# First stage of a two-layer transformer kernel: two batches ahead of the attention, two along with it

## The chip, the cores and the metric

The kernel runs on one core of a Trainium2 chip. The metric is the device time of one execution in microseconds (us). Before the change it is 1527.2 us, the median of three runs (1524.87 to 1527.45). A measurement of this kind tells about 0.2%, some 3 us, from no change.

PE is the matrix engine, DVE the vector engine, ACT the activation engine, POOL the general engine; SP only issues DMAs here. Each runs its own instructions strictly in order, and they wait for each other by semaphores. PSUM holds eight banks of 512 fp32 per partition, and PE writes there; DVE and ACT read from there.

## The reference

Input x is 4 batches x 1024 tokens x 128. Two transformer layers follow; layer 0 is the one that the change touches:

```python
xn = _ln(x, g_attn, b_attn)
qkv = (xn @ qkv_w + qkv_b)          # 16 heads of 8
scores = einsum('bhqd,bhkd->bhqk', q, k) / sqrt(8)
scores = where(causal, -inf, scores)
attn = einsum('bhqk,bhkd->bhqd', softmax(scores), v)
attn = attn @ out_w + out_b
x = x + attn
# 8 steps of a recurrence with tanh, a second norm, a gelu feed-forward, a linear part,
# then layer 1: attention without a mask, and a relu feed-forward; a norm after each part
```

All of it is computed in fp32 accuracy. For the score products q and k are therefore split in three bf16 parts each.

## The kernel before, in words

**Stages.** The first stage makes q, k and v of layer 0. For each batch it has six steps, in `FIRST_STEPS`: *norm* (DVE takes the statistics of 8 tiles of 128 tokens, `L495`, `L499`), *scale* (POOL takes the root of the variance, `L508` to `L519`; ACT then scales half of the tiles, `L526`, and DVE the other half, `L533`), *turn* (PE transposes, `L545`; ACT copies with gain and bias, `L617`), *q* and *k* (PE multiplies, `L552`; ACT writes the first bf16 part, `L620`, `L625`; DVE the remainder in fp32, `L633`; ACT the second part, `L623`, `L628`; DVE the third, `L638`) and *v* (PE, `L560`, and DVE adds the bias, `L657`). The k product waits for the remainder of q, the v product for that of k, since both use the same bank. SP writes the parts to HBM (`scr_q`, `scr_k`, `L604`), and later loads them in another layout, four heads at a time (`load_group`, `L113`, 14 DMAs: a *load*). There are 16 loads a layer: a batch has four groups of four heads. A load waits until its batch is written.

**Attention.** A group of layer 0 has 20 units. A *max* unit is a score product on PE (`L383`, with the mask's product `L389`) and its row maximum on DVE (`L324`). They run 24 units ahead. When the maxima of half a group's queries are complete, POOL splits them (`L265` to `L271`), PE transposes (`L436`), ACT copies (`L309`), and SP stores them to HBM and loads them as further rows of Q (`L230`, `L235`): that is *turn_max*. A *key* unit is the score product again, keys by queries with the maxima subtracted within the product (`L404`), and the exponential on ACT (`L296`). POOL cuts the diagonal blocks (`L280`). *weigh* multiplies with v (`L426`), *turn_out* transposes back and divides (`L443`, `L342`, `L345`).

**PSUM.** Two of the eight banks collect the weighed values. The other six are a ring of three slots of two banks (`RING`). Each max, key, turn_max and turn_out takes the next slot, and its PE instruction waits in `slot_free` until the entry that had the slot has been read out. The first stage does not use the ring: batch b has slot b (`bank[b]`), the fourth being the two banks of the weighed values.

**Order.** `Program` gives each entry a tick; all engines walk through the same sorted list and take out what is theirs. Before: batch b's step i has tick b + i, then come load 0, 1 and 2, then the attention of layer 0, one key unit a tick. The last ticks of layer 0 have the first steps of the middle stage among them. Batches 1 and 2 of the first stage work in the buffer `shared`, 0 and 3 in `own`. The attention needs `shared` for its exponentials.

## Time and profile before

| | |
|---|---|
| median of the runs | 1527.2 us |
| profiled execution | 1526.45 us |
| its span, first to last instruction | 1524.7 us |
| busy PE / DVE / ACT / POOL | 90% / 82% / 71% / 18% |
| mean granted PE clock | 0.966 |

The times of the rows below count from the start of the span. A row of the order in time is one instruction or several alike in a row; idle time stands in brackets with what ended it. PE's busy time is modelled, since its products overlap. The granted clock is a share of 2.4 GHz; 0.50 is 1.2 GHz. An fp32 product is counted as two instructions (two products of 512 columns are x4).

### The profile page before, as it was taken

The page shows a single profiled execution, that of the slowest core. Times are in us where ns is not written, and L with a number is a line of the kernel's source. Part 1 is how long each engine was busy: PE and PEld are TensorE (multiplying, and loading weights), DVE is VectorE, ACT ScalarE, POOL GpSimd, SP SyncE. Part 2 cuts the span into 40 slices and gives each one's busy share as a digit, 9 for nine tenths or more (in the row PEclk, how much of TensorE's full clock was granted, in tenths as well). Part 3 has the DMA queues.
Part 4 walks back from the last instruction along what each step waited for, and adds up shares of the span by engine and source line. Part 5 has one row for each costly group of instructions (what it writes and reads, how often), then busy time and mean ns, then how long its engine had stood idle before and what let it go on. Part 6 is the DMA issues. An engine that isn't in the chain of part 4 may idle for free.

```text
span 1524.7 us, 31977 instructions
## 1 busy us (share of the span) xinstructions
PE 1369.9 (90%) x13016; PEld 565.3 (37%) x13016; DVE 1249.3 (82%) x1715; ACT 1081.6 (71%) x1239; POOL 278.1 (18%) x624
## 2 busy tenths in 40 slices
PE   6699999999998768888679999999999999999886
PEld 3333434343343334446423333233333333233355
DVE  7978888888885387885989999999999999997143
ACT  6167777777777657764358888888888888887642
POOL 4021322223133132332200000000000000001252
PEclk9689999999999899999889999999999999999998
DMA  5610110101100000012120000000000000000001
GB/s 177 168 45 24 31 38 25 45 24 42 27 4 3 1 1 0 1 65 82 42 64 23 23 24 23 14 17 18 23 23 23 23 23 23 3 3 3 1 15 42
DMA packets 38995, 47.90 MB, mean 31 GB/s; under 512 B 11072, under 2 KB 20160, under 8 KB 38720
## 3 DMA queue, kind: packets, MB, share of 16 engines
q1 hardware_dynamic: 38416, 45.31, 10.1%
q8 instruction: 103, 1.69, 0.4%
q10 hardware_dynamic: 432, 0.53, 0.1%
q14 instruction: 44, 0.36, 0.1%
HBM read 30.22 MB, written 15.47 MB: 30 GB/s over the span
## 4 chain that ended last, share of the span: by engine, by line
PE 62%; DVE 23%; ACT 6%; issue 4%; POOL 3%; SPq 1%; DMA 1%; POOLq 0%; ACTq 0%; DVEq 0%
PE ps L426 22%; DVE l_negp L324 14%; PE ps L404 12%; PE ps L383 12%; PE ps L552 7%; ACT shared L296 3%; PE ps L443 2%; PE ps L389 2%; POOL n_rs L514 2%; DVE n_bst L495 2%; PE ps L545 1%; PE ps L1040 1%; SPq L113 1%; PE ps L908 1%; PE ps L560 1%
## 5 line engine op out<-in xcount | busy, mean ns | idle before, releaser
L324 DVE TENSOR_REDUCE l_negp<-ps 128x2 f32<-128x1024 f32 (+2 forms) x832 | 953.3, 1181 | 75.5 <-PE ps L389 36.4
L296 ACT ACTIVATE shared<-ps 128x1024 f32<-128x1024 f32 (+1 forms) x832 | 820.4, 991 | 196.8 <-PE ps L404 168.1
L426 PE MATMUL ps<-shared,l_vs 128*32 128x256 f32 (+3 forms) x6648 | 515.3, 386 | 4.1 <-POOL shared L280 3.3
L383 PE MATMUL ps<-Ks,Qs 48*128 48x512 bf16 (+3 forms) x1792 | 329.9, 369 | 40.6 <-DVE l_negp L324 27.2
L404 PE MATMUL ps<-Qs,Ks 51*128 51x512 bf16 (+3 forms) x1792 | 320.8, 366 | 25.5 <-ACT shared L296 10.7
L404 PEld LDWEIGHTS ps<-Qs,Ks 51*128 51x128 bf16 x1792 | 81.3, 93 | 330.6 <-issue 159.3
L426 PEld LDWEIGHTS ps<-shared,l_vs 128*32 128x32 f32 x6648 | 134.8, 108 | 172.3 <-issue 141.7
L383 PEld LDWEIGHTS ps<-Ks,Qs 48*128 48x128 bf16 x1792 | 87.6, 94 | 194.3 <-ACT shared L296 91.0
L280 POOL TENSOR_SCALAR_AFFINE_SELECT shared<-shared 128x512 f32<-128x512 f32 x128 | 81.7, 639 | 321.0 <-ACT shared L296 320.9
L265 POOL CAST l_parts<-l_negm 128x16 bf16<-128x16 f32 x64 | 12.6, 197 | 441.8 <-DVE l_negm L329 438.6
L389 PE MATMUL ps<-mask,id 64*128 64x128 bf16 x1024 | 69.2, 223 | 0.0
L552 PE MATMUL ps<-shared,w_sb 128*128 128x512 f32 x120 | 60.8, 639 | 7.6 <-ACT shared L998 5.7
L514 POOL TENSOR_TENSOR n_rs<-n_ve,neg_half 128x4 f32<-128x4 f32 x56 | 62.7, 1120 | 4.4
L552 PE MATMUL ps<-own,w_sb 128*128 128x512 f32 x120 | 61.1, 635 | 2.2 <-DVE attn_tm L849 1.8
L389 PEld LDWEIGHTS ps<-mask,id 64*128 64x128 bf16 x1024 | 50.2, 99 | 21.0 <-issue 2.1
L251 POOL COPY l_vs<-v_tm 128x256 f32<-128x256 f32 x32 | 12.7, 397 | 232.7 <-PE ps L426 199.8
L508 POOL TENSOR_TENSOR n_ve<-n_mv,eps 128x4 f32<-128x4 f32 x56 | 12.2, 218 | 215.4 <-DVE n_mv L499 215.4
L342 DVE RECIPROCAL l_rc<-ps 128x16 f32<-128x16 f32 x64 | 16.5, 257 | 39.7 <-PE ps L443 39.1
L309 ACT ACTIVATE l_msp<-ps 48x128 bf16<-48x128 bf16 x64 | 17.3, 270 | 39.6 <-PE ps L436 39.5
L824 DVE SCALAR_TENSOR_TENSOR own<-own 128x1024 f32<-128x1024 f32 x16 | 19.5, 1219 | 31.1 <-ACT own L767 31.1
L443 PE MATMUL ps<-ident,l_outT 128*128 128x128 f32 x256 | 41.8, 286 | 2.5 <-ACT l_outT L302 2.5
L552 PE MATMUL ps<-own,wx 128*128 128x512 f32 x56 | 31.9, 699 | 12.0 <-DVE own L824 11.8
(160 smaller groups left out, 1090.4 us busy)
## 6 DMA issues: line engine op xcount, KB each, us to landing
Qs<-scr_q SPq DMA_DIRECT2D x128, 64.0 KB
Ks<-scr_k SPq DMA_DIRECT2D x64, 96.0 KB
Qs<-scr_q SPq DMA_DIRECT2D x128, 32.0 KB
Ks<-scr_k SPq DMA_DIRECT2D x64, 64.0 KB
scr_q<-own SPq DMA_DIRECT2D x4, 768.0 KB, 3.6
scr_q<-shared SPq DMA_DIRECT2D x4, 768.0 KB, 3.5
scr_k<-own SPq DMA_DIRECT2D x4, 768.0 KB, 5.0
scr_k<-shared SPq DMA_DIRECT2D x4, 768.0 KB, 4.8
```

What stands on the lines that cost most here:

```text
L280: pool.affine_select(out=blk, in_=blk, compare_op=ALU.is_ge, fill=0.0, base=0, pattern=[[0, GH], [1, P]], channel_multiplier=-1).then_inc( ...
L296: act.activation(dst, src, ACT.Exp, scale=SCALE).then_inc(exped, 1)
L324: dve.tensor_reduce(dst, src, AX_X, ALU.max, negate=True).then_inc(reduced, 1)
L383: last = pe.matmul(outs[par], Qs[s][r:r + MROW, h2, qt * P:(qt + 1) * P], Ks[s][r:r + MROW, h2, at:at + w], start=True, stop=True)
L389: last = pe.matmul(outs[par][:, w - P:w], id2[r:r + ROWS, j, :], mask2[r:r + ROWS, j, :], start=False, stop=True, skip_group_check=True)
L404: last = pe.matmul(to[:, par, i * w:(i + 1) * w], Ks[s][r:r + MROW + 3, h2, kt * P:(kt + 1) * P], Qs[s][r:r + MROW + 3, h2, qh * CH + lo:( ...
L426: last = pe.matmul(pv_ps[q % 2][32 * h:32 * h + 32, a:a + wide], vs[g % 2][:, kt, h, :], pT[m % PRING][:, h, a:a + wide], start=m == u.fir ...
L443: last = pe.transpose(to[:, t * P:(t + 1) * P], outT[:, t * P:(t + 1) * P], ident)
L495: last = dve.bn_stats(self.bst[:, b, t, :], src[:, t * P:(t + 1) * P])
L514: pool.tensor_tensor(self.rs[:, b, of], self.ve[:, b, of], self.norms.neg_half[:, of], ALU.pow)\
L552: last = pe.matmul(bank[:, i * CH:(i + 1) * CH], weight, src[:, i * CH:(i + 1) * CH], start=start, stop=True, skip_group_check=not start)
L824: dve.scalar_tensor_tensor(out=then, in0=u[b], scalar=DT * DT / BETA ** (k + 1), in1=then, op0=ALU.mult, op1=ALU.add).then_inc(moved[b % 2 ...
```

## The change

Batches 0 and 1 are made ahead of the attention, batch 1 two ticks behind batch 0. Batches 2 and 3 are made within it: their six steps have the ticks 60, 64, 68, 72, 76, 80 and 120, 124, ... 140 of the attention of layer 0, each ahead of the attention's entries of that tick. Tick 60 is the first key unit of group 3, tick 120 that of group 6; batch 2's first load is asked for at tick 106, batch 3's at 186. The four PSUM results of a batch (turn, q, k, v) take a slot of the ring each, in turn. All batches work in the two halves of `own`: batch 2 waits until batch 0's are written. A group's load of three groups on is issued at its seventh key unit instead of its first.

```diff
-            if entry[1] == u.first_unit[g] and g % NGRP + 3 < NGRP:
+            if entry[1] == u.first_unit[g] + 6 and g % NGRP + 3 < NGRP:
...
+        if place.before[entry][0] == "first":
+            _, name, b = place.before[entry]
+            if name == "turn":
+                pe.wait_ge(handed.x_ready, b + 1)
+            elif name == "v":
+                pe.wait_ge(handed.v_made[0], b + 1)
+            else:
+                pe.wait_ge(handed.rest["qk".index(name)], b + 1)
+            return
...
-    xT = [work[b][:, 3, :] for b in range(B)]
-    parts = [parts_of(work[b]) for b in range(B)]
+    xT = [work[b % 2][:, 3, :] for b in range(B)]
+    parts = [parts_of(work[b % 2]) for b in range(B)]
...
+            if b >= 2:
+                act.wait_ge(v_mm, b - 1)
             act.wait_ge(n_turned, b + 1)
-            act.activation(xT[b], bank[b], ACT.Identity, bias=C("b_attn"), scale=C("g_attn")).then_inc(x_ready, 1)
+            act.activation(xT[b], bank_of("first", name, b), ACT.Identity, bias=C("b_attn"), scale=C("g_attn")).then_inc(x_ready, 1)
         elif name == "q":
+            if b >= 2:
+                act.wait_ge(written[b - 2], 32)
...
     def tensor(pe, name, b):
+        if name in FIRST_BANKS:
+            bank_free(pe, ("first", name, b))
...
+FIRST_AT = {2: 60, 3: 120}
...
-        out = [(b + i, 0, -b, ("first", name, b)) for i, name in enumerate(FIRST_STEPS) for b in range(B)]
-        at = len(FIRST_STEPS) + B
+        out = [(2 * b + i, 0, -b, ("first", name, b)) for i, name in enumerate(FIRST_STEPS) for b in range(2)]
+        at = len(FIRST_STEPS) + 4
...
+        out += [(at + FIRST_AT[b] + 4 * i, 0, 0, ("first", name, b)) for i, name in enumerate(FIRST_STEPS)
+                for b in range(2, B)]
...
-            elif entry[0] in ("key", "max", "turn_max", "turn_out"):
+            elif entry[0] in ("key", "max", "turn_max", "turn_out") or entry[0] == "first" and entry[1] in FIRST_BANKS:
```

On DVE, the last instructions of the first stage and the first reduce, before (`L633` remainder, `L638` third part, `L657` v):

```order
L633 SCALAR_TENSOR_TENSOR attn_tm<-ps,c_sb,own 128x1024
L638 TENSOR_TENSOR shared<-attn_tm,shared 128x1024
L633 SCALAR_TENSOR_TENSOR v_tm<-ps,c_sb,shared 128x1024
L638 TENSOR_TENSOR shared<-v_tm,shared 128x1024
L657 TENSOR_TENSOR v_tm<-ps,r_sb 128x1024
L638 TENSOR_TENSOR own<-attn_tm,own 128x1024
L633 SCALAR_TENSOR_TENSOR v_tm<-ps,c_sb,own 128x1024
L638 TENSOR_TENSOR shared<-v_tm,shared 128x1024
L657 TENSOR_TENSOR v_tm<-ps,r_sb 128x1024
L638 TENSOR_TENSOR own<-v_tm,own 128x1024
L657 TENSOR_TENSOR v_tm<-ps,r_sb 128x1024
L324 TENSOR_REDUCE l_negp<-ps 128x2x2 x2
```

and with the change, where `L643`, `L648` and `L667` are the same three:

```order
L643 SCALAR_TENSOR_TENSOR v_tm<-ps,c_sb,own 128x1024
L643 SCALAR_TENSOR_TENSOR attn_tm<-ps,c_sb,own 128x1024
L648 TENSOR_TENSOR own<-v_tm,own 128x1024
L667 TENSOR_TENSOR v_tm<-ps,r_sb 128x1024
L648 TENSOR_TENSOR own<-attn_tm,own 128x1024
L643 SCALAR_TENSOR_TENSOR v_tm<-ps,c_sb,own 128x1024
L648 TENSOR_TENSOR own<-v_tm,own 128x1024
L667 TENSOR_TENSOR v_tm<-ps,r_sb 128x1024
L324 TENSOR_REDUCE l_negp<-ps 128x2x2 x2
```

Of the work of four batches that of two is left ahead of the first reduce.

On PE, around the seventeenth unit of group 3, before (`L404` key, `L383` max, `L389` mask, `L426` weigh; `l_reduced` counts DVE's maxima, `exped` ACT's exponentials):

```order
L426 MATMUL ps<-shared,l_vs 32x256 [waits exped]
L426 MATMUL ps<-shared,l_vs 32x256 x3
L404 MATMUL ps<-Qs,Ks 128x384 [waits l_reduced]
L404 MATMUL ps<-Qs,Ks 128x384
L383 MATMUL ps<-Ks,Qs 128x128 [waits exped,loaded0_1]
L383 MATMUL ps<-Ks,Qs 128x128
L389 MATMUL ps<-mask,id 128x128 x4
L383 MATMUL ps<-Ks,Qs 128x128 x2
L389 MATMUL ps<-mask,id 128x128 x4
L426 MATMUL ps<-shared,l_vs 32x256 x4
L404 MATMUL ps<-Qs,Ks 128x384 [waits l_reduced]
L404 MATMUL ps<-Qs,Ks 128x384
```

and with the change (`L411`, `L390`, `L396`, `L433` are these, `L555` is the k product of batch 2; `q_rest0` and `k_rest0` count DVE's remainders):

```order
L555 MATMUL ps<-own,w_sb 128x512 [waits q_rest0,l_reduced]
L555 MATMUL ps<-own,w_sb 128x512
L411 MATMUL ps<-Qs,Ks 128x384 [waits exped]
L411 MATMUL ps<-Qs,Ks 128x384
L390 MATMUL ps<-Ks,Qs 128x128 [waits l_reduced,loaded0_1]
L390 MATMUL ps<-Ks,Qs 128x128
L396 MATMUL ps<-mask,id 128x128 x4
L390 MATMUL ps<-Ks,Qs 128x128 x2
L396 MATMUL ps<-mask,id 128x128 x4
L433 MATMUL ps<-shared,l_vs 32x256 x4
L411 MATMUL ps<-Qs,Ks 128x384 [waits k_rest0]
L411 MATMUL ps<-Qs,Ks 128x384
```

The k product stands in one slot of the ring, and the second key product behind it waits for DVE's remainder of k.

On ACT, in the first units of group 3, before (`L296` exponential, `L302` copy of the weighed values, `L309` maxima):

```order
L296 ACTIVATE shared<-ps 128x2x384 [waits weighed,keyed] x2
L302 ACTIVATE l_outT<-ps 128x512 [waits l_out_turned,weighed]
L296 ACTIVATE shared<-ps 128x2x2x256 [waits weighed,keyed]
L296 ACTIVATE shared<-ps 128x2x2x128 [waits weighed,keyed]
L309 ACTIVATE l_msp<-ps 48x128 [waits l_max_stored,l_max_turned]
```

and with the change, where `L529` is the scaling of batch 2 and `n_shifted` counts POOL's results:

```order
L296 ACTIVATE shared<-ps 128x2x384 [waits weighed,keyed] x2
L302 ACTIVATE l_outT<-ps 128x512 [waits l_out_turned,weighed]
L529 ACTIVATE attn_tm<-x_tm,n_shift,n_rs 128x128 [waits n_shifted]
L529 ACTIVATE attn_tm<-x_tm,n_shift,n_rs 128x128 x3
L296 ACTIVATE shared<-ps 128x2x2x256 [waits weighed,keyed]
L296 ACTIVATE shared<-ps 128x2x2x128 [waits weighed,keyed]
L309 ACTIVATE l_msp<-ps 48x128 [waits l_max_stored,l_max_turned]
```

The exponentials of the fifth and sixth unit come behind a wait for POOL.

## Rows read from the trace of the kernel before

**Rows 1.** Page, part 2: PE and its granted clock, tenths, 40 slices.
```profile
PE   6699999999998768888679999999999999999886
...
PEclk9689999999999899999889999999999999999998
```

**Rows 2.** Busy time by stretch: us, us on each engine (instructions), clock, DMA.
```profile
60.00:74.00 14.00, 9.41 (x81) 3.81 (x75) 13.96 (x15) 0.27 (x1) 0.83 (x4) 0.50 0.51 85
100.00:126.77 26.77, 25.31 (x338) 10.66 (x334) 23.02 (x26) 20.10 (x25) 7.06 (x17) 1.00 0.11 33
```

**Rows 3.** PE in order of time: start, us, what, idle time before.
```profile
17.89 3.62 PE L552 MATMUL ps<-own,w_sb 128*128 128x512 f32 x4
...
47.50 0.29 PE L383 MATMUL ps<-Ks,Qs 48*128 48x128 bf16 x2
...
74.05 0.61 PE L404 MATMUL ps<-Qs,Ks 51*128 51x512 bf16 x2 [1.27 <-DMA Qs<-scr_m]
...
103.39 0.39 PE L404 MATMUL ps<-Qs,Ks 51*128 51x512 bf16 x2
...
210.49 0.39 PE L404 MATMUL ps<-Qs,Ks 51*128 51x512 bf16 x2
```

**Rows 4.** SP's queue in order of time, start of the program.
```profile
35.14 0.36 SPq L604 DMA_DIRECT2D scr_k<-own  x1
39.88 3.09 SPq L113 DMA_DIRECT2D Qs<-scr_q  x8
...
66.54 0.32 SPq L230 DMA_DIRECT2D scr_m<-l_msp  x1
```

**Rows 5.** DVE in order of time, the first row maxima.
```profile
49.58 5.81 DVE L324 TENSOR_REDUCE l_negp<-ps 128x4 f32<-128x512 f32 x6
```

**Rows 6.** Groups by line, 0 to 49.5 us: busy, mean ns; idle before.
```profile
L514 POOL TENSOR_TENSOR n_rs<-n_ve,neg_half 128x4 f32<-128x4 f32 x8 | 8.1, 1014 | 0.6
...
L495 DVE BATCH_NORM_STATS2 n_bst<-x_tm 128x6 f32<-128x128 f32 x32 | 6.8, 278 | 1.4 <-DMA x_tm<-in_x 1.4
L526 ACT ACTIVATE attn_tm<-x_tm,n_shift,n_rs 128x128 f32<-128x128 f32 x16 | 6.6, 482 | 7.6 <-POOL n_shift L519 7.6
...
L657 DVE TENSOR_TENSOR v_tm<-ps,r_sb 128x1024 f32<-128x1024 f32 x4 | 4.9, 1225 | 0.4
L533 DVE TENSOR_SCALAR attn_tm<-x_tm,n_mv,n_rs 128x128 f32<-128x128 f32 x16 | 4.8, 364 | 0.0
...
L499 DVE BATCH_NORM_AGGREGATE n_mv<-n_bst 128x2 f32<-128x6 f32 x32 | 3.0, 158 | 0.3
...
L633 DVE SCALAR_TENSOR_TENSOR attn_tm<-ps,c_sb,own 128x1024 f32<-128x1024 f32 x2 | 2.6, 1279 | 3.4 <-ACT own L620 3.4
...
L638 DVE TENSOR_TENSOR own<-attn_tm,own 128x1024 bf16<-128x1024 f32 x2 | 2.4, 1216 | 0.0
...
L620 ACT ACTIVATE own<-ps,c_sb 128x1024 bf16<-128x1024 f32 x2 | 2.2, 1113 | 3.0 <-PE ps L552 3.0
...
L508 POOL TENSOR_TENSOR n_ve<-n_mv,eps 128x4 f32<-128x4 f32 x8 | 1.6, 206 | 4.4 <-DVE n_mv L499 4.4
```

**Rows 7.** ACT in order of time, batch 0's normalized tokens transposed.
```profile
14.84 1.20 ACT L617 ACTIVATE own<-ps,c_sb 128x1024 f32<-128x1024 f32 x1 [0.45 <-PE ps L545]
```

**Rows 8.** PE in order of time, two key products in mid group.
```profile
227.09 0.39 PE L404 MATMUL ps<-Qs,Ks 51*128 51x512 bf16 x2
...
228.32 0.39 PE L404 MATMUL ps<-Qs,Ks 51*128 51x512 bf16 x2
```

**Rows 9.** DVE in order of time, the same place.
```profile
227.86 4.96 DVE L324 TENSOR_REDUCE l_negp<-ps 128x2 f32<-128x1024 f32 x4 [0.27 <-PE ps L383]
```

**Rows 10.** PE in order of time, products of the middle stage within attention.
```profile
473.87 1.09 PE L545 MATMUL ps<-ident,attn_tm 128*128 128x128 f32 x8
...
478.72 1.98 PE L552 MATMUL ps<-own,w_sb 128*128 128x512 f32 x4
```

**Rows 11.** Groups by line of ACT, 0 to 520 us: table loads.
```profile
L526 ACT ACT_TABLE_LOAD x1 | 1.3, 1283 | 2.2 <-issue 2.2
```

More of the change, by code:

```diff
@@ L285, in scalar @@
             g, m, pairs = u.key_unit[entry[1]]
-            lo, layer = u.step[m][3], g // NGRP
-            if entry[1] == u.first_unit[layer * NGRP]:
-                act.wait_ge(handed.written[layer][1], 32)
-                act.wait_ge(handed.written[layer][2], 32)
-                act.wait_ge(handed.v_mm[layer], 3)
+            lo = u.step[m][3]
+            if entry[1] == u.end[0]:
+                act.wait_ge(handed.written[1][1], 32)
+                act.wait_ge(handed.written[1][2], 32)
+                act.wait_ge(handed.v_mm[1], 3)
             act.wait_ge(keyed, entry[1] + 1)
@@ L361, in slot_free @@
             pe.wait_ge(normed, i + 1)
-        elif kind == "first":
-            pe.wait_ge(handed.v_made[0], i + 1)
         elif kind == "mid":
@@ L594, in first_stage @@
     ln = RowNorm(ctx, nc, norms, 0)
-    n_turned, x_ready = sem("n_turned"), sem("x_ready")
-    s_mm, s_first, s_rest, s_second = ([sem(f"{s}_{n}") for s in "qk"] for n in "mm first rest second".split())
+    n_turned, x_ready, s_rest = sem("n_turned"), handed.x_ready, handed.rest
+    s_mm, s_first, s_second = ([sem(f"{s}_{n}") for s in "qk"] for n in "mm first second".split())
     s_parted, v_mm, v_made, written = handed.parted[0], handed.v_mm[0], handed.v_made[0], handed.written[0]
@@ L615, in scalar @@
                 act.wait_ge(small_in, 32)
+            if b >= 2:
+                act.wait_ge(v_mm, b - 1)
             act.wait_ge(n_turned, b + 1)
-            act.activation(xT[b], bank[b], ACT.Identity, bias=C("b_attn"), scale=C("g_attn")).then_inc(x_ready, 1)
+            act.activation(xT[b], bank_of("first", name, b), ACT.Identity, bias=C("b_attn"), scale=C("g_attn")).then_inc(x_ready, 1)
         elif name == "q":
+            if b >= 2:
+                act.wait_ge(written[b - 2], 32)
             act.wait_ge(s_mm[0], b + 1)
-            act.activation(parts[b][:, 0, 0, :], bank[b], ACT.Identity, bias=C("bq0")).then_inc(s_first[0], 1)
+            act.activation(parts[b][:, 0, 0, :], bank_of("first", name, b), ACT.Identity, bias=C("bq0")).then_inc(s_first[0], 1)
         elif name == "k":
@@ L624, in scalar @@
             act.wait_ge(s_mm[1], b + 1)
-            act.activation(parts[b][:, 1, 0, :], bank[b], ACT.Identity, bias=C("bk0")).then_inc(s_first[1], 1)
+            act.activation(parts[b][:, 1, 0, :], bank_of("first", name, b), ACT.Identity, bias=C("bk0")).then_inc(s_first[1], 1)
         elif name == "v":
@@ L632, in left @@
             dve.wait_ge(s_first[s], b + 1)
-            dve.scalar_tensor_tensor(out=rest[s][b], in0=bank[b], scalar=C(("bq0", "bk0")[s]), in1=parts[b][:, s, 0, :],
+            dve.scalar_tensor_tensor(out=rest[s][b], in0=bank_of("first", name, b), scalar=C(("bq0", "bk0")[s]), in1=parts[b][:, s, 0, :],
                                      op0=ALU.add, op1=ALU.subtract).then_inc(s_rest[s], 1)
@@ L656, in vector @@
             dve.wait_ge(s_parted[1], b + 1)
-            dve.tensor_tensor(rows(v[b]), rows(bank[b]), R("bv0").unsqueeze(1).to_broadcast([P, QT, P]), ALU.add)\
+            dve.tensor_tensor(rows(v[b]), rows(bank_of("first", name, b)), R("bv0").unsqueeze(1).to_broadcast([P, QT, P]), ALU.add)\
                 .then_inc(v_made, 1)
     def tensor(pe, name, b):
+        if name in FIRST_BANKS:
+            bank_free(pe, ("first", name, b))
         if name == "turn":
             ln.wait_scaled(pe, b)
-            turn_batch(pe, bank[b], n_tm[b], ident).then_inc(n_turned, 1)
+            turn_batch(pe, bank_of("first", name, b), n_tm[b], ident).then_inc(n_turned, 1)
         elif name in ("q", "k"):
@@ L1091, in __init__ @@
         held, had, at = {}, [None] * (RING + 1), 0
-        ends = {"first": FIRST_STEPS[-1], "mid": MID_STEPS[-1], "last": LAST_STEPS[-1]}
+        ends = {"mid": MID_STEPS[-1], "last": LAST_STEPS[-1]}
         for entry in self.order:
@@ L1172, in two_layer_kernel @@
         wx_of = [W("x")] + [wx[:, k, :] for k in range(ITERS - 1)]
-        first = first_stage(nc, ctx, W, C, R, scr[0:2], work, bank, handed, x_in, x_tm, v_tm, attn_tm, ident[:, :], norms,
-                            small_in, w_first_in)
         attn, clear_values, clear_maxima, bank_free, evacuated, v_copied = attention(
@@ L1177, in two_layer_kernel, with bank_of @@
             mask2, id2, ident_bf[:, :], halved, pT, ps)
+        def bank_of(*entry):
+            return bank[program.slot[entry]]
+        first = first_stage(nc, ctx, W, C, R, scr[0:2], [own[:, 0], own[:, 1]], bank_of, bank_free, handed, x_in, x_tm, v_tm,
+                            attn_tm, ident[:, :], norms, small_in, w_first_in)
         def free_for(of):
```

26 lines of the change are left out of this document (13 added, 13 removed).

## Prediction

> **What bounds the kernel now.** I read the page's slices first, then busy time by stretch, then the order in time on each engine, then the costs by line. They show the granted TensorE clock low only in the second and third slice, near the start (0.6 and 0.8), and PE at 9 tenths with a full clock in the long flat parts [rows 1]. The stretches say what kind of work each part is. From 60 to 74 us DVE is busy 13.96 of 14 us and PE 9.41 at a granted clock of 0.50: the row maxima that run ahead of the first key product are DVE's. From 100 us on, one group of four heads takes 26.77 us, with PE busy 25.3, DVE 23.0, ACT 20.1 and POOL 7.1 [rows 2]. There no engine is free: PE has 1.5 us left, DVE 3.7, ACT 6.7. The reader should keep this in mind, since the change puts work exactly there.
>
> The front, before that, is a chain of its own. Batch 0's last part of k is written out by SP at 35.14, its landing lets SP begin the 14 DMAs of load 0 at 39.88, and the first max product starts on PE at 47.50 [rows 3, 4]. DVE gets to the first reduce only at 49.58, and its row shows no idle time ahead: it has worked for the other batches until then [rows 5]. Then DVE reduces without a pause worth the name until the first key product at 74.05, for which PE waited 1.27 us more, because the stored maxima were behind loads 1 and 2 in SP's queue until 66.54 [rows 3, 4].
>
> **What the change takes away in front.** Two batches fewer are made before the first max. By line, the statistics cost DVE (6.8 + 3.0)/4 = 2.45 us a batch, its half of the scaling 4.8/4 = 1.2, two remainders 2 x 1.28, two third parts 2 x 1.22, the v add 1.22: 9.9 us a batch [rows 6]. But 2 x 9.9 = 19.8 us is not the gain, for DVE will now wait. What is late next is batch 0's own chain. Its q product ran from 17.89 and took 3.62 us for 4 instructions, behind batch 1's transposes; x transposed had been ready at 14.84 + 1.20 = 16.0 [rows 3, 7]. In the new order q stands ahead of them, and DVE's half of the scaling no longer stands behind batch 1's statistics, so I start q at 15.3. Then: q product 3.5, first part on ACT 1.1, remainder on DVE 1.3, k product 1.9 (at full clock) to 3.6 (at half), ACT 1.1, DVE 1.3, second part on ACT 1.1, third on DVE 1.2, hand-overs about 0.5 [rows 3, 6]. That is 28.3 to 30; a q product at full speed would give 26.6. I take 28.5, against 35.1. From the write of k to the first max I keep 47.50 - 35.14 = 12.4 us, since it is the same three steps on SP and the DMA queue: 40.9. The first reduce follows at about 41.8, 7.8 us earlier (6.3 to 10 by the ends above). DVE is done with batch 1 near 36 us and idles till then.
>
> From there to the first key it is 74.05 - 49.58 - 1.27 = 23.2 us of reduces, unchanged: 65.0. Would SP be in time? From the start of load 0 to the write of the maxima it took 66.54 - 39.88 = 26.7 us, with three loads and five writes, and the maxima were there 7.5 us later. Load 0 now starts 6.6 us earlier, at 33.3: at the same pace the key would have its maxima at 67.5, 2.5 us late. But three of the five writes are gone from that stretch, so I take them as in time, and the 1.27 us as gone too. **Gain in front: 9.1 us** (5.5 to 11.5). The loads moved from the first unit of a group to its seventh have about 30 units till their first reader; I cost them at nothing, and being past a `turn_max` they can only help the stored maxima. If that cover were gone, one load's issue would show, under 26.7/3 = 8.9 us.
>
> **What it puts into the attention.** Each of batches 2 and 3 brings six steps, four units apart. A unit is one key, one max and one weigh: 228.32 - 227.09 = 1.23 us on PE, and in that part four reduces fill 4.96 us of DVE, so both are full [rows 8, 9]. The ring has three slots, so a slot is wanted again after one and a half units. Each step costs what it holds back the next unit:
> - q: PE product 1.9 (4 instructions took 1.98 in the same surroundings at 478.72 [rows 10]), then ACT 1.1, then DVE 1.3: the slot is free after 4.3 us, and PE has only the key, max and weigh of one unit (1.25) to do meanwhile. The second key product after it is 3.0 late, and the reduces 3.4, as DVE stands in order behind the remainder. Queued behind it: everything, since PE, ACT and DVE are all in order.
> - k: the same, 3.0; the second part of q (priced as its first, 1.1) and the third lie beside the product.
> - v: the product 1.9 runs beside ACT's 1.1 and DVE's third part, then the add: 1.1 + 1.2 + 1.2 = 3.5, less one unit: 2.3.
> - turn: PE 1.0 (eight transposes took 1.09 at 473.87 [rows 10]), its copy on ACT 1.2 just misses: 1.2.
> - norm: 2.45 on DVE with no product beside it, less the idle there: 1.5.
> - scale: on ACT it waits for POOL, whose row is a root of 1.01 and three small operations of 0.2 behind the mask of the last unit: 1.8, and then 4 x 0.48, partly overlapped, 1.65 [rows 6]; the next exp is 3.5 late, DVE's 1.2 lies in it: 3.3.
>
> Sum 14.3 us a batch. Bounds: if every idle moment of the group could be filled, DVE would set it: 23.0 + 9.9 - 26.8 = 6.1 a batch. If nothing lay beside anything, 4.3 + 5.4 + 3.5 + 2.2 + 2.45 + 4.7 = 22.5. I take 13.7, near the walk, with a little made up between the steps: **27.4 us for two batches** (12 to 45). A function switch on ACT I cost at nothing: Identity, Copy and Exp follow one another from 2.2 us on with one table load up to 520 us [rows 11].
>
> The profiled execution took 1526.45 us with a span of 1524.7, just under the median of 1527.2. **1526.45 - 9.1 + 27.4 = 1544.8, so 1545 us.** With gains of 5.5 to 11.5 and costs of 22 to 31 its own range is 1537 to 1552.
>
> **Rivals.**
> The holes take the work (cost at its floor). PE, DVE and ACT all have idle time, and the four-unit spacing may let it be used. Then 1526.45 - 9.1 + 12.2 = 1529.5. Against it: the slots are three, and a delay seen by PE is not made up in a ring that is full. Chance 0.11.
>
> The delays vanish, and it is faster. PE's busy time is modelled, so its real room may be more than 1.5 us a group; if later groups ran faster than 26.8 until the delay was gone, two batches would cost less than the 9.1 they free; at 3 us it ends at 1520. It decides below 4.5 us a batch. For it: group 0 ran 11 us at half clock and still took only 103.39 - 74.05 = 29.3 us [rows 3]. Against: full-clock groups keep the same distance, (210.49 - 103.39)/4 = 26.77, set by waits in turn on three engines, with nothing that stores a lead. Chance 0.07. The Trainium skill speaks for this one (Perfetto Trace Analysis, Optimization Strategy: where the most-contended engine changes over time, interleaving those regimes may improve performance; and Identifying the Most-Contended Engine: matmul busy time is no measure of how near the roofline PE is). The trace agrees on the first half only: the regimes differ in front, yet the one that receives the work has DVE at 86%. By that rule the sum would be 1520, by the rows it is 1545.
>
> The clock falls. With the pauses PE's share in the two stretches drops to about 32 of 40 us; at 60 to 74 us, with 9.4 of 14, it had half clock [rows 2]. If two stretches of 35 us ran so, each pays some 3 times the 2.6 us that group 0 lost in 11 us at half clock, 16 in all: 1561. Against: in the middle stage PE is at 6 to 8 tenths in several slices, and the clock there stays at 0.8 or above [rows 1]. Chance 0.10. The Trainium skill has a rule for it (TensorE: Matmul & The Clock Gate, A second HAM failure mode: psum-queue depth-cycling), that small pauses between groups of products, from cycling PSUM banks, can make the clock swing; no row of full-clock attention here shows it yet.
>
> **How the numbers follow.** Forecast 0.72, floor 0.11, faster 0.07, clock 0.10. The range 1531 to 1554 leaves out the faster case, about half of the floor case, most of the clock case and the tails: 0.2. A measurement of this kernel can tell about 0.2%, 3 us, from no change; the floor case straddles that. Faster by over 0.2%: 0.08; within: 0.07; slower: 0.85.
>
> **What would show it.** First max product near 41 us and DVE idle before it; first key near 65; groups 3 and 6 (with the step v just behind) 39 to 42 us long instead of 26.8, all others unchanged; in them PE waiting behind q and k for the DVE remainder, and ACT waiting for POOL at the scaling. I am wrong if those groups take under 33 us, if the first key comes later than 68, or if the clock row drops in slices 4 to 7.

## The result and the profile after

| | before | after |
|---|---|---|
| median of the runs | 1527.1 us | 1557.6 us (1555.0 to 1559.2) |
| ratio, 95% interval | | 1.0204 (1.0187 to 1.0220) |
| profiled execution, its span | 1526.45, 1524.7 us | 1559.21, 1557.5 us |
| mean granted PE clock | 0.966 | 0.950 |

The change makes the kernel 30.5 us slower. 1545 was forecast: the sign is right, the time lies 3.6 us above the range.

The page's part 2 of the kernel after answers to [rows 1]: PE and its granted clock in 40 slices of 39 us.

```profile
PE   4799898899999867898769999999999999999886
...
PEclk9599898999999989999869999999999999999998
```

Slices 5 and 7 have a clock digit of 8 where [rows 1] has 9. These are the two stretches that got the moved steps, and this is what the prediction named as proof against it.

**The front.** PE in order of time (start, us, what, idle time before), answering to [rows 3]; in the kernel after, `L390` is the max product, `L411` the key product:

```profile
15.56 3.75 PE L555 MATMUL ps<-own,w_sb 128*128 128x512 f32 x4 [1.45 <-ACT own L625]
...
40.55 0.29 PE L390 MATMUL ps<-Ks,Qs 48*128 48x128 bf16 x2 [4.65 <-DMA Ks<-scr_k]
...
65.51 0.61 PE L411 MATMUL ps<-Qs,Ks 51*128 51x512 bf16 x2 [0.65 <-DVE l_negp L324]
...
75.58 0.61 PE L411 MATMUL ps<-Qs,Ks 51*128 51x512 bf16 x2
```

DVE and SP's queue in order of time, answering to [rows 5] and [rows 4]:

```profile
41.41 0.69 DVE L324 TENSOR_REDUCE l_negp<-ps 128x4 f32<-128x512 f32 x1 [4.25 <-PE ps L396]
```

```profile
32.82 3.08 SPq L113 DMA_DIRECT2D Qs<-scr_q  x8
...
53.77 0.32 SPq L230 DMA_DIRECT2D scr_m<-l_msp  x1
```

The first max product starts at 40.55 us (40.9 forecast), DVE had been idle for 4.25 us, the maxima leave SP's queue at 53.77, long before the key product needs them, and that starts at 65.51 (65.0 forecast). By the seventh key product of group 0 (75.58, against 84.03 before) 8.5 us are gained.

**The two groups.** Busy time by stretch, answering to [rows 2]: us, then us on each engine (instructions), clock, DMA. Each group is cut at its seventh key product. First come group 3 and the first six units of group 4, then group 5, which got nothing, then group 6 and the first six units of group 7:

```profile
148.49:162.05 13.56, 9.62 (x100) 3.73 (x100) 10.55 (x30) 7.58 (x12) 6.75 (x16) 0.81 0.02 3
162.05:192.69 30.64, 26.42 (x264) 11.94 (x264) 20.46 (x22) 19.38 (x22) 4.35 (x8) 0.92 0.17 54
192.69:201.18 8.49, 7.44 (x101) 3.29 (x101) 8.06 (x11) 5.78 (x7) 3.15 (x9) 1.00 0.26 96
...
219.84:227.95 8.11, 7.51 (x101) 3.28 (x101) 6.86 (x10) 5.99 (x8) 3.42 (x10) 1.00 0.02 5
227.95:246.60 18.65, 17.79 (x232) 7.38 (x232) 16.15 (x18) 14.14 (x16) 3.65 (x9) 1.00 0.16 45
...
246.60:259.33 12.73, 9.03 (x100) 3.90 (x100) 10.15 (x30) 7.58 (x12) 6.46 (x16) 0.87 0.02 5
259.33:292.44 33.11, 28.73 (x264) 12.91 (x264) 20.93 (x22) 19.40 (x22) 4.58 (x9) 0.85 0.15 50
292.44:300.93 8.49, 7.44 (x101) 3.29 (x101) 8.06 (x11) 5.78 (x7) 3.15 (x9) 1.00 0.26 96
```

Group 5 took 8.11 + 18.65 = 26.76 us, as every group did before. Group 3 has 13.56 + 30.64 + 8.49 where 34.88 is usual: 17.8 too much. Group 6 has 19.4 too much. Together 37.2 us, where 27.4 were forecast. In both groups the clock is below 1.00 in the stretches that hold the moved steps, and full again behind them.

PE in order of time through group 3 (`L433` is weigh, `L555` the q or k product):

```profile
152.46 0.34 PE L411 MATMUL ps<-Qs,Ks 51*128 51x384 bf16 x2 [1.06 <-DVE l_negp L324]
...
153.59 0.50 PE L411 MATMUL ps<-Qs,Ks 51*128 51x384 bf16 x2 [0.58 <-DVE l_negp L324]
...
154.45 1.08 PE L433 MATMUL ps<-shared,l_vs 128*32 128x256 f32 x8
...
160.02 0.28 PE L411 MATMUL ps<-Qs,Ks 51*128 51x128 bf16 x4 [2.02 <-ACT shared L296]
...
171.75 0.64 PE L433 MATMUL ps<-shared,l_vs 128*32 128x256 f32 x8
...
174.08 1.98 PE L555 MATMUL ps<-own,w_sb 128*128 128x512 f32 x4
...
178.65 0.39 PE L411 MATMUL ps<-Qs,Ks 51*128 51x512 bf16 x2 [1.48 <-DVE attn_tm L643]
...
186.90 0.34 PE L411 MATMUL ps<-Qs,Ks 51*128 51x384 bf16 x2 [1.34 <-DVE v_tm L643]
```

ACT at the scaling and behind q, and DVE at the same two places:

```profile
157.41 1.65 ACT L529 ACTIVATE attn_tm<-x_tm,n_shift,n_rs 128x128 f32<-128x128 f32 x4 [1.98 <-POOL n_shift L522]
...
176.16 1.11 ACT L630 ACTIVATE own<-ps,c_sb 128x1024 bf16<-128x1024 f32 x1 [1.79 <-PE ps L555]
```

```profile
158.66 1.16 DVE L536 TENSOR_SCALAR attn_tm<-x_tm,n_mv,n_rs 128x128 f32<-128x128 f32 x4 [2.65 <-POOL n_rs L517]
...
177.31 1.28 DVE L643 SCALAR_TENSOR_TENSOR attn_tm<-ps,c_sb,own 128x1024 f32<-128x1024 f32 x1 [2.73 <-ACT own L630]
```

All waits that the prediction named are there: PE behind DVE's statistics (152.46), behind ACT and so POOL (160.02), behind the remainders of q and k (178.65, 186.90). One thing is there that the sum did not have. The same eight weigh products take 1.08 us at 154.45 and 0.64 at 171.75. In group 3 PE works at half clock, the 1.2 GHz level, in two stretches:

```profile
153.60:157.00 3.40, 3.40 (x32) 1.46 (x36) 2.41 (x3) 1.35 (x3) 2.73 (x8) 0.50 0.02 5
...
160.40:167.20 6.80, 6.72 (x56) 2.79 (x57) 3.96 (x6) 2.87 (x4) 0.92 (x2) 0.50 0.06 16
```

The first follows PE's two waits for DVE, the second the wait behind ACT and POOL; between them the clock is full. Group 6 has the same two, from 252.5 and from 259.4 us, and a third from 269.6.

**The rest of the program**, from the first key product of group 15, the last of layer 0, before and then after:

```profile
480.64:1524.70 1044.06, 939.22 (x7849) 378.03 (x7848) 842.45 (x1198) 751.01 (x840) 149.40 (x311) 0.97 0.07 22
```

```profile
509.38:1557.50 1048.12, 945.40 (x7849) 382.94 (x7848) 841.83 (x1198) 751.66 (x840) 149.66 (x311) 0.96 0.07 22
```

The account of the two profiled executions is thus -8.5 in front, +37.2 in the two groups, +4.1 behind them: 32.8 us. The last item has the same instructions on both sides. In three kernels below that do not differ there either, the same stretch took 1044.1 (experiment 2), 1047.6 (experiment 7, the first) and 1047.9 us (experiment 1), so it varies between executions by as much and is not counted as an effect. The medians differ by 30.5.

### The profile page after: what moved, and what is told of

Same layout as the page of the kernel before. It is cut to its first block, busy times and chain, and to the rows that moved or that the text cites. A ratio compares the mean times of both kernels' runs of the same rounds, so it can differ in the third digit from the quotient of the medians.

```text
span 1557.5 us, 31991 instructions
## 1 busy us (share of the span) xinstructions
PE 1387.5 (89%) x13016; PEld 573.0 (37%) x13016; DVE 1248.6 (80%) x1715; ACT 1082.9 (70%) x1239; POOL 281.7 (18%) x624
## 4 chain that ended last, share of the span: by engine, by line
PE 61%; DVE 24%; ACT 6%; POOL 4%; issue 4%; DMA 1%; SPq 0%; POOLq 0%; ACTq 0%; DVEq 0%
PE ps L433 21%; DVE l_negp L324 15%; PE ps L411 12%; PE ps L390 12%; PE ps L555 8%; ACT shared L296 4%; PE ps L450 2%; POOL n_rs L517 2%; PE ps L548 2%; PE ps L396 2%; DVE n_bst L498 2%; PE ps L1053 1%; PE ps L921 1%; PE ps L563 1%; DVE n_mv L502 1%
## 5 line engine op out<-in xcount | busy, mean ns | idle before, releaser
L296 ACT ACTIVATE shared<-ps 128x1024 f32<-128x1024 f32 (+1 forms) x832 | 821.1, 992 | 204.4 <-PE ps L411 177.2
L433 PE MATMUL ps<-shared,l_vs 128*32 128x256 f32 (+3 forms) x6648 | 518.2, 388 | 4.3 <-POOL shared L280 3.5
L390 PE MATMUL ps<-Ks,Qs 48*128 48x512 bf16 (+3 forms) x1792 | 333.3, 373 | 41.8 <-DVE l_negp L324 23.5
L411 PE MATMUL ps<-Qs,Ks 51*128 51x512 bf16 (+3 forms) x1792 | 322.6, 368 | 39.4 <-ACT shared L296 14.1
L411 PEld LDWEIGHTS ps<-Qs,Ks 51*128 51x128 bf16 x1792 | 81.4, 93 | 348.1 <-issue 158.2
L433 PEld LDWEIGHTS ps<-shared,l_vs 128*32 128x32 f32 x6648 | 135.3, 108 | 174.9 <-issue 144.1
L390 PEld LDWEIGHTS ps<-Ks,Qs 48*128 48x128 bf16 x1792 | 87.9, 94 | 194.6 <-ACT shared L296 89.4
L555 PE MATMUL ps<-own,w_sb 128*128 128x512 f32 x136 | 70.8, 649 | 4.6 <-DVE attn_tm L862 1.8
L396 PE MATMUL ps<-mask,id 64*128 64x128 bf16 x1024 | 71.2, 228 | 0.0
L555 PE MATMUL ps<-shared,w_sb 128*128 128x512 f32 x104 | 53.0, 641 | 7.9 <-ACT shared L1011 5.7
L396 PEld LDWEIGHTS ps<-mask,id 64*128 64x128 bf16 x1024 | 51.4, 101 | 22.8 <-issue 4.0
L251 POOL COPY l_vs<-v_tm 128x256 f32<-128x256 f32 x32 | 13.7, 427 | 230.6 <-PE ps L433 199.7
L309 ACT ACTIVATE l_msp<-ps 48x128 bf16<-48x128 bf16 x64 | 17.3, 271 | 44.2 <-PE ps L443 44.2
L555 PE MATMUL ps<-own,wx 128*128 128x512 f32 x56 | 33.2, 725 | 11.8 <-DVE own L837 11.8
```

The lines of the kernel that those rows point to most:

```text
L296: act.activation(dst, src, ACT.Exp, scale=SCALE).then_inc(exped, 1)
L390: last = pe.matmul(outs[par], Qs[s][r:r + MROW, h2, qt * P:(qt + 1) * P], Ks[s][r:r + MROW, h2, at:at + w], start=True, stop=True)
L396: last = pe.matmul(outs[par][:, w - P:w], id2[r:r + ROWS, j, :], mask2[r:r + ROWS, j, :], start=False, stop=True, skip_group_check=True)
L411: last = pe.matmul(to[:, par, i * w:(i + 1) * w], Ks[s][r:r + MROW + 3, h2, kt * P:(kt + 1) * P], Qs[s][r:r + MROW + 3, h2, qh * CH + lo:( ...
L433: last = pe.matmul(pv_ps[q % 2][32 * h:32 * h + 32, a:a + wide], vs[g % 2][:, kt, h, :], pT[m % PRING][:, h, a:a + wide], start=m == u.fir ...
L555: last = pe.matmul(bank[:, i * CH:(i + 1) * CH], weight, src[:, i * CH:(i + 1) * CH], start=start, stop=True, skip_group_check=not start)
```

## The experiments

Three accounts of the 37.2 us stood against each other. *Serial*: my walk, only sized too low, with the POOL wait on the path. *Clock*: the pauses bring PE to half clock, and everything in the stretch pays. *Holds*: q, k and v keep their slots while ACT and DVE read them in turn. Each kernel below changes one thing, and was timed in alternation with the kernel before, to which its ratio refers.

**1. Statistics and scaling of batches 2 and 3 ahead of the attention; only their products stay in it.** Edit of the kernel after:

```diff
-                for b in range(2, B)]
+                for b in range(2, B) if i >= 2]
+        out += [(2.5, 0, 0, ("first", "norm", 2)), (3.2, 0, 0, ("first", "scale", 2)),
+                (3.3, 0, 0, ("first", "norm", 3)), (7.5, 0, 0, ("first", "scale", 3))]
```

> The changed kernel, but the steps norm and scale of batches 2 and 3 are done ahead of the attention (within the first stage's idle time on DVE, ACT and POOL); turn, q, k and v stay at their places in groups 3 and 6. In the changed kernel the first six keys of these two groups, which hold norm and scale, are 5.4 and 4.6 us longer than the 8.1 of others, and PE's granted clock is 0.81 to 0.92 there. Theory clock (the pauses of norm and scale also bring the granted clock down to half, and that makes the following products longer): 10 us of pauses and 6 to 9 us of slow products go, the clock in groups 3 and 6 is 1.00, the two batches cost about 19 us instead of 37, some 1540 us in all. Rival serial (the cost is only the chain of waits of each step, at whatever clock): only the 10 us go, less 1 us in front: 1548.

Measured: 1543.8 us, ratio 1.0117 (1.0082 to 1.0152), so 13.7 us less than the kernel after, and between the two forecasts. The stretches behind the sixth unit of groups 3 and 6:

```profile
154.88:185.62 30.74, 25.83 (x266) 11.37 (x265) 21.01 (x22) 19.36 (x22) 4.87 (x9) 0.94 0.17 54
247.66:276.60 28.94, 24.30 (x264) 11.16 (x264) 20.91 (x22) 19.36 (x22) 4.89 (x9) 1.00 0.19 57
```

The first six units are regular again, and the first key product is no later (65.15 us): in front the two steps lie in the time in which DVE and ACT wait for batch 0's loads. Of the 14.1 us by which the two groups are shorter, 10.1 lie in the first six units and the rest behind them, where no instruction was touched. At full clock the four products of a batch cost 28.94 - 18.65 + 0.37 = 10.7 us. Group 3 isn't at full clock, though: at 171.7 us, behind a wait of 1.48 us for the remainder of q, PE falls to half clock once more, and the stretch is 1.8 us longer than that of group 6. So the waits behind the products can bring the clock down too.

**2. POOL takes the root two and a half units earlier.** In the kernel after, POOL starts on it only at the scaling, behind the mask of the last unit. Edit:

```diff
-        if name == "scale":
+        if name == ("scale" if b < 2 else "root"):
             ln.root(pool, b)
...
+        out += [(at + FIRST_AT[b] + 1.5, 0, 0, ("first", "root", b)) for b in range(2, B)]
```

> The changed kernel, but POOL's root for batches 2 and 3 stands 2.5 units ahead of ACT's scaling, right behind DVE's statistics, instead of at the same tick. ACT waited 1.98 us for POOL there and DVE 2.65. Theory clock: those waits go, 4 us in two batches, and if the remaining pauses are too short to bring the clock down, 5 to 8 us more: 1546 to 1550, with the clock near 1.00 in groups 3 and 6. Rival serial: 4 us, 1553.5, whatever the clock does. If the statistics' pause alone brings the clock down, the clock stays at 0.8 to 0.9 and the time at 1553.5 under both.

Measured: 1548.2 us, ratio 1.0129 (1.0103 to 1.0155): 9.4 less by medians, more than the 4 us of the serial forecast. The profiled execution is the fastest of four (1542.6 us; the others took 1547.4 to 1549.9, at a mean clock of 0.957 against 0.962), so its rows show this kernel at its best. Groups 3 and 6:

```profile
146.79:157.38 10.59, 7.60 (x100) 3.24 (x100) 10.45 (x30) 7.46 (x12) 6.33 (x16) 1.00 0.02 4
157.38:186.28 28.90, 24.30 (x264) 11.16 (x265) 20.87 (x22) 19.36 (x22) 4.64 (x9) 1.00 0.18 57
...
240.19:250.83 10.64, 8.79 (x100) 3.87 (x100) 10.39 (x30) 7.46 (x12) 6.06 (x16) 0.84 0.02 6
250.83:279.77 28.94, 24.30 (x264) 11.16 (x264) 20.91 (x22) 19.36 (x22) 4.89 (x9) 1.00 0.19 57
```

Against the kernel after, 11.0 us are gone from the two groups, of which 5.9 behind the sixth unit, where no instruction was touched: 30.64 + 33.11 against 28.90 + 28.94. In the first six units 13.56 and 12.73 became 10.59 and 10.64: some 2.1 us each is what ACT had waited for POOL (1.98), all that the serial account has, and 0.9 in group 3 is left, which I put to the clock as well. So 6.8 of the 11.0 us go to the clock, now 1.00 in three of the four stretches (by medians it is 9.4 - 4.2 = 5.2); in the fourth, at 0.84, it costs nothing, since PE is not what sets those six units. These four rows also give the price of the steps at full clock: 10.59 - 8.11 = 2.5 us for statistics and scaling without the wait for POOL, and 10.25 + 0.37 = 10.6 for the products. With the wait I take 2.5 + 2.1 = 4.6 us, which no run shows at full clock (the kernel after has it in group 6, 12.73 - 8.11, at 0.87). That is 15.2 a batch in the form of the change.

**3. Only the pauses.** All four batches are made ahead as before; statistics and scaling of batches 2 and 3 are repeated at the ticks of the change, into the same buffer, with the same values. Nothing else is moved. Edit of the kernel before, its core (the second kernel has the root at the tick shown, the first at that of the scaling):

```diff
+        for b, t in ((2, 60), (3, 120)):
+            out += [(at + t, 0, 0, ("first", "again", b)), (at + t + 1.5, 0, 0, ("first", "root_again", b)),
+                    (at + t + 4, 0, 0, ("first", "scale_again", b))]
```

> The kernel before, all four batches in front, with the statistics and the scaling of batches 2 and 3 done a second time at the places where the change has them (ticks 60 and 64, 120 and 124 of layer 0), over the same normalized values, which nobody reads any more. POOL's root stands at the scaling's tick, as in the change. No product is moved. Theory clock: the waits bring PE's granted clock to half, and the 27 us of groups 3 and 6 become 5 us longer by the waits (as the first six keys of the changed kernel, 5.4 and 4.6) and 3 to 5 us more by slow products after them: 16 to 20 us in all, 1544 to 1547, clock row below 0.9 in these groups. Rival serial: 10 us, 1537, clock 1.00.

> As the kernel with the repeated statistics and scaling, but POOL's root stands 2.5 units ahead of the scaling, so that ACT and DVE do not wait for it. Theory clock: the pauses are 2.5 us a batch (first six keys 10.6 instead of 8.1) and too short to bring the clock down: 5 us, 1532, clock at 1.00 or nearly. Rival serial: the same 2.5 us plus nothing, so the difference to the kernel without the early root is 4 us by serial waits and 11 to 14 by the clock theory.

Measured: 1542.5 us, ratio 1.0080 (1.0056 to 1.0104), with the root late; 1532.4 us, ratio 1.0020 (1.0003 to 1.0037), with it early. Groups 3 and 6, root late and then early:

```profile
156.50:170.07 13.57, 10.50 (x102) 4.05 (x101) 10.57 (x30) 7.58 (x12) 6.75 (x16) 0.68 0.22 62
170.07:190.37 20.30, 19.69 (x232) 7.79 (x232) 15.94 (x18) 14.11 (x16) 3.11 (x8) 0.88 0.01 3
243.92:256.66 12.74, 9.02 (x101) 3.90 (x101) 10.17 (x30) 7.58 (x12) 6.41 (x16) 0.87 0.25 66
256.66:279.02 22.36, 21.63 (x232) 8.14 (x231) 16.39 (x18) 14.14 (x16) 3.39 (x9) 0.77 0.01 3
```

```profile
156.14:166.73 10.59, 7.61 (x101) 3.24 (x101) 10.45 (x30) 7.45 (x12) 6.33 (x16) 1.00 0.24 67
166.73:186.87 20.14, 19.16 (x233) 7.75 (x233) 16.22 (x18) 14.10 (x16) 3.40 (x9) 0.92 0.04 9
240.43:251.02 10.59, 8.83 (x101) 3.87 (x100) 10.39 (x30) 7.46 (x12) 6.05 (x16) 0.84 0.30 79
251.02:269.69 18.67, 17.81 (x234) 7.39 (x233) 16.17 (x18) 14.12 (x16) 3.65 (x9) 1.00 0.02 3
```

This is the run that shows the clock's part. Without one product of the first stage in the groups, the pauses alone cost 15.4 us in the profiled execution (14.0 by medians), and the clock falls by itself. In the first kernel the rows behind the sixth unit hold nothing but ordinary attention, and are 1.6 and 3.7 us too long at 0.88 and 0.77. The early root takes 10.1 us off by medians, where the serial account has some 4. It doesn't save the clock everywhere: in group 3 it falls at 167.8 us, and the row behind the sixth unit is 1.5 us too long. Now it adds up: -8.5 in front, +15.4 for the pauses with their clock, + 2 x 10.6 for the products at full clock: +28.1, and the change measured -8.5 + 37.2 = +28.7 there.

**4. Only the products.** Turn, q, k and v of a batch are computed once more in the attention, each in a slot of the ring at the ticks of the change, and nobody reads them (so no output depends on them). Edit of the kernel before, its core:

```diff
+        for b, t in ((0, 60), (3, 120)):
+            out += [(at + t + 8 + 4 * i, 0, 0, ("repeat", name, b)) for i, name in enumerate(("turn", "q", "k", "v"))]
...
+        if place.before[entry][0] == "repeat":
+            return
```

> The kernel before, with all four batches in front, and PE's four products of one batch (turn, q, k, v) issued again at ticks 68, 72, 76, 80 and 128 to 140 of layer 0, each into the next slot of the ring. Nobody reads the results (the copies, remainders and parts of ACT and DVE are left out of the repetition), so the slot is free at once. With its readers a batch of products costs 10.6 us at full clock. Theory holds (most of it is slots held for ACT and DVE): the bare 6.7 us of PE, less some of the 1.5 us of idle time a group, 5 to 6 us a batch, 1538. Rival (PE's work is the cost, readers are hidden): 9 to 10.6 a batch, 1547.

Measured: 1538.6 us, ratio 1.0064 (1.0048 to 1.0081): 10.5 us by medians, 5.2 a batch. Groups 3 and 4, each whole; groups 6 and 7 took the same:

```profile
154.85:188.19 33.34, 31.57 (x363) 14.49 (x363) 23.79 (x27) 20.37 (x25) 7.36 (x18) 1.00 0.10 28
188.19:214.68 26.49, 25.14 (x331) 10.66 (x331) 22.55 (x26) 19.85 (x23) 6.81 (x17) 1.00 0.12 32
```

The clock stays full, and by these rows a batch costs 33.34 + 26.49 - 2 x 26.77 = 6.3 us. This is the figure to set beside the 10.6, which is from the same stretches: 6.3 are PE's own work, and 4.3 come with the readers, by slots held and ACT's and DVE's time. By medians the split is 5.2 and 5.4. PE around the repeated q product, where a key, a max, a weigh and the second key now follow without a wait:

```profile
172.47 1.98 PE L566 MATMUL ps<-own,w_sb 128*128 128x512 f32 x4
174.38 0.39 PE L406 MATMUL ps<-Qs,Ks 51*128 51x512 bf16 x2
174.61 0.38 PE L385 MATMUL ps<-Ks,Qs 48*128 48x512 bf16 x2
174.92 0.64 PE L428 MATMUL ps<-shared,l_vs 128*32 128x256 f32 x8
175.49 0.39 PE L406 MATMUL ps<-Qs,Ks 51*128 51x512 bf16 x2
```

**5. The slot given back a step earlier.** For batches 2 and 3, ACT copies the q and k product in full to SBUF; first part and remainder are then made from the copy, and PE waits only for the copy. Edit of the kernel after, its core:

```diff
+            act.activation(rest[s][b], src, ACT.Identity, bias=bias).then_inc(handed.full[s], 1)
+            act.wait_ge(handed.full[s], b - 1)
+            act.activation(parts[b][:, s, 0, :], rest[s][b], ACT.Copy).then_inc(s_first[s], 1)
```

> The changed kernel, but for q and k of batches 2 and 3 ACT first copies the product with its bias to SBUF in fp32 (which frees the slot of the ring), then makes the first bf16 part from the copy, and DVE subtracts from the copy. The slot is held 1.9 + 1.1 us instead of 1.9 + 1.1 + 1.3; ACT has 1.05 us more for each. My walk (the slot held until DVE's remainder stops PE): PE's waits of 1.48 and 1.34 us behind q and k go, four times, 5 us: 1552.5. Rival (ACT, in order, takes over as the one that stops PE, since its exponentials come 1.05 us later): no change, 1556 to 1559. The clock at the norm's place stays as it is under both.

Measured: 1558.9 us, ratio 1.0208 (1.0186 to 1.0229): no gain. PE behind q (`L392` is the max product here):

```profile
175.66 0.39 PE L413 MATMUL ps<-Qs,Ks 51*128 51x512 bf16 x2 [0.16 <-ACT attn_tm L623]
177.65 0.39 PE L392 MATMUL ps<-Ks,Qs 48*128 48x512 bf16 x2 [1.61 <-ACT shared L296]
```

The wait for the remainder went from 1.48 to 0.16 us, and the very next instruction waits 1.61 us for ACT, whose exponential now stands behind two passes. The belief that DVE's remainder alone stops PE fell: ACT in its order takes the place. The clock was also lower here behind the sixth units (0.83 and 0.86, against 0.92 and 0.85), so the two times alone would not tell; but PE's idle time in these stretches, span less busy, did not shrink either: 5.1 + 4.6 us, against 4.2 + 4.4 in the kernel after.

**6. The loads at the first unit of a group again.** Edit of the kernel after:

```diff
-            if entry[1] == u.first_unit[g] + 6 and g % NGRP + 3 < NGRP:
+            if entry[1] == u.first_unit[g] and g % NGRP + 3 < NGRP:
```

> The changed kernel with the loads issued again at the first unit of a group, as in the kernel before. I cost the moved loads at nothing: 1556 to 1559, as the changed kernel. Rival (the loads stand in SP's queue ahead of the stored maxima or of the writes of batches 2 and 3, and the move was needed): over 3 us slower than the changed kernel.

Measured: 1556.4 us, ratio 1.0171 (1.0146 to 1.0196), the interval overlapping that of the kernel after. That part of the change costs nothing, as forecast.

**7. All four batches ahead, but batch 0 favoured.** If the front is 8.5 us shorter once batch 0 is served first, can it be had without moving anything into the attention? Two orders; edits of the kernel before, the first spacing the batches two ticks apart, the second only taking batch 0 first within a tick:

```diff
-        out = [(b + i, 0, -b, ("first", name, b)) for i, name in enumerate(FIRST_STEPS) for b in range(B)]
-        at = len(FIRST_STEPS) + B
+        out = [(2 * b + i, 0, -b, ("first", name, b)) for i, name in enumerate(FIRST_STEPS) for b in range(B)]
+        at = len(FIRST_STEPS) + 2 * B
```

```diff
-        out = [(b + i, 0, -b, ("first", name, b)) for i, name in enumerate(FIRST_STEPS) for b in range(B)]
+        out = [(b + i, 0, b, ("first", name, b)) for i, name in enumerate(FIRST_STEPS) for b in range(B)]
```

> The kernel before, with all four batches ahead of the attention, each in its own slot, but two ticks apart instead of one, so that batch 0's chain goes first. Nothing of the attention is changed. In the changed kernel the first max could start at 40.6 us with DVE idle from 37.2; here DVE should fill that time and be done with four batches near 46 us instead of 49.6, since its 39.4 us of work start at 6.4. Theory (the front is DVE's work plus its idle time ahead of it): 3 to 4 us faster, 1523.5. Rival (the writes and loads on SP's queue set the first key anyway, 74.05 before): within 1 us of 1527.

> The kernel before, one tick between batches as there, but at an equal tick the earlier batch's step comes first. Two ticks apart cost 5.4 us in front, since too few chains were open to fill DVE. Here four chains stay open: theory (DVE is filled as before, batch 0's part gets written earlier, first key unchanged): within 2 us of 1528. Rival (the order in which later batches go first is what fills the waits of ACT and POOL): 2 to 5 us slower.

Measured: 1532.9 us, ratio 1.0038 (1.0025 to 1.0051), and 1531.5 us, ratio 1.0030 (1.0015 to 1.0045): both a little slower. In the first, DVE's first reduce:

```profile
55.57 1.81 DVE L324 TENSOR_REDUCE l_negp<-ps 128x4 f32<-128x512 f32 x2
```

DVE starts its reduces at 55.57 us instead of 49.58, and the first key product follows at 79.42 (before: 74.05). In the second kernel it is at 76.67. With all four batches ahead, DVE's work for them has to be done before the first reduce in any order, and the two new orders have it done later: the first reduce is at 55.57 us in the first and at 52.83 in the second. The old order was the better one.

**8. DVE relieved in front by POOL.** POOL makes the third part of q of batches 1 to 3. Edit of the kernel before, its core:

```diff
+        elif name == "k" and b:
...
+            pool.tensor_tensor(parts[b][:, 0, 2, :], rest[0][b], parts[b][:, 0, 1, :], ALU.subtract)\
+                .then_inc(s_parted[0], 1)
```

> The kernel before, with the third bf16 part of q of batches 1 to 3 made by POOL instead of DVE (POOL is idle there). My reading of the front is that DVE's work sets it from 22.8 us to the first key at 74.05: three times 1.22 us less on DVE gives 3.6 us, 1523.5. Rival (SP's loads or the chains of the last batches take over, or POOL slows DVE down): within 1 us of 1527.

Measured: 1529.8 us, ratio 1.0000 (0.9983 to 1.0017). The first key product starts at 72.69 us, 1.4 earlier, although DVE was relieved of 3 x 1.22 us; its first reduce comes only 1.0 us earlier (48.58), behind 1.28 us of waiting for PE. POOL in order of time:

```profile
41.96 2.93 POOL L612 TENSOR_TENSOR own<-attn_tm,own 128x1024 bf16<-128x1024 f32 x1
```

The pass takes 2.1 to 2.9 us there against 1.22 on DVE, and 1.4 us cannot be told from nothing in the medians. In the traces it is hardly more: in experiments 3 and 4, whose front is that of the kernel before, the first key product starts at 73.02 to 73.73 us.

**9. The maxima run 22 units ahead instead of 24 in layer 0.** The front holds 24 units of maxima before the first key; two fewer should shorten it. Edit of the kernel before:

```diff
-        ahead = longest + 10
+        ahead = longest + (10 if layer else 8)
```

> The kernel before, with the max units of layer 0 running 22 units ahead instead of 24. In front DVE alone works through them, 1.02 us each, while ACT stands still; at the end of the layer the last units run without maxima. If the maxima still come in time (7 units between turn_max and its key become 5, 6.7 us, against 1.4 + 2.9 us of DMA), the front is 2 us shorter and the end of the layer 0.8 us longer: 1527, 1 to 1.5 us faster than before. Rival: keys wait for the stored maxima in each group, 0.5 us or more each, 1535 and above.

Measured: 1605.3 us, ratio 1.0505 (1.0487 to 1.0523): 77 us slower, where I had expected a gain of 1 to 1.5. PE at the seventh key unit of group 4, where the second half of a group's queries begins to need its maxima, and the waits by sum from 100 to 400 us (us in total, times, longest):

```profile
212.99 0.61 PE L404 MATMUL ps<-Qs,Ks 51*128 51x512 bf16 x2 [2.34 <-DMA Qs<-scr_m]
```

```profile
PEld ps L404 <- DMA Qs<-scr_m: 29.1, 9, 3.8
```

In each of the nine groups in these 300 us the seventh key unit waits for the stored maxima, up to 3.8 us. The two units were the cover of the way by POOL, PE, ACT, SP and HBM. The clock was 0.83 in that stretch and 0.921 over the kernel. The nine groups took 300.5 us instead of 240.9, twice the 29.1 us of the waits themselves, so one pause a group costs far more than itself. Two of the nine, at a clock of 0.94, took 30.6 and 30.7 us, the other seven 33.6 to 34.5. That puts roughly half of the loss to the clock, as an estimate; no run separated it.

No version beats the kernel before; of the changed line the best is the first, 1543.8 us.

## Why the prediction was wrong in size and right in sign

- **Front.** Right: 8.5 us for a forecast of 9.1. q started at 15.56 (15.3), the first max at 40.55 (40.9), the first key at 65.51 (65.0), DVE idle ahead of its first reduce, the stored maxima in time. Of some 20 us of DVE work taken out of the front, under half came back, because batch 0's own chain was late next.
- **Loads moved to the seventh unit.** Right: nothing (experiment 6).
- **The four products.** Walked as 3.0 + 3.0 + 2.3 + 1.2 = 9.5 us a batch; 10.6 at full clock (experiments 1 and 2). Right but for 1.1 us. The walk named the remainder as what frees the slot; experiment 5 showed that ACT's order stands right behind it.
- **Norm and scale.** Walked as 1.5 + 3.3 = 4.8, with the wait for POOL. Measured: 2.5 at full clock without that wait (experiment 2), and 4.6 with it at a clock of 0.87. Right.
- **The step that failed** is "I take 13.7, near the walk", as the price of a batch: it was 18.6. The walk itself (14.3) holds at full clock, where the steps cost 15.2 by the estimate in experiment 2; the "little made up between the steps" was not there (2 x 1.5 = 3.0 us of the miss). The larger part is that nearly all rows from which it was made are at full clock, and the sum took that clock to hold. Experiment 3 shows that the pauses of *norm* and *scale* bring it down with nothing else moved, and experiment 2 that it comes back for the most part when a wait of 2 us is taken out: 6.8 us in the profiled executions, 5.2 by medians. 3.0 + 6.8 is the 9.8 by which the forecast of the two groups was low. The two parts are not independent measurements: the 6.8 is what is left when the waits are taken off.
- **The rival that came true** is "the clock falls", given 0.10 and priced at 16 us, 1561. It has the place and the sign, and is nearer to the result than the forecast; its size was more than twice too large, since PE was at half clock in parts of the stretches only (0.81, 0.92, 0.87, 0.85), and 6.8 us came of it on top of the walk. Its price was also taken from 11 us at half clock in group 0 before; by the clock of 0.78 over that group's 29.34 us it was 12.9, which makes it some 14 us instead of 16. The argument against it, that the middle stage keeps 0.8 or above at 6 to 8 tenths, was read the wrong way: 0.8 in a slice of 39 us *is* a loss of clock, and a tenth of it on a PE-bound stretch of 40 us is 4 us. [rows 1] has such an 8 in four slices behind the front, which the prediction's first paragraph passes over. The Trainium skill (TensorE: Matmul & The Clock Gate, A second HAM failure mode: psum-queue depth-cycling) describes small pauses between groups of products that make the clock swing. The trace now agrees that such pauses, here of 0.6 to 2.0 us and caused by waits for DVE and ACT, go with a swinging clock.
- **The floor and the faster rival** are refuted: no later group ran below 26.7 us, so no delay was made up. The Trainium skill (Perfetto Trace Analysis, Optimization Strategy) says that interleaving regimes may improve performance. Here it did not: what gave 8.5 us when it left the DVE-bound front cost 37.2 in the attention.
- **What is left**: the 4.1 us behind the groups, which differ between executions of kernels alike there.

What starts the fall is open in part. The second fall, from 160.4 and 259.4 us, follows the wait that comes from POOL in both groups (160.02, and 257.93 with 1.70 us), and with the root early neither group has it. The first fall comes ahead of that wait, behind PE's waits of 1.06 and 0.58 us for DVE. With the root early PE has the same two waits in both groups, and the clock stays full in group 3 and falls in group 6. So POOL's wait can't be what began the first fall, and the two waits for DVE don't always bring it. No run took the pause of the statistics away and left that of POOL.
